# A 7x7 dynamic convolution by frequencies: three image chunks in place of five, four products for 52 frequencies, and the first filter layer applied to the image

## What is computed

```python
key = einsum('bchw,oc->bohw', x, K_w) + K_b              # 49 maps
key = softmax(key.reshape(b, 49, hw).transpose(0, 2, 1), axis=1)   # over pixels
filters = einsum('bcn,bnk->bck', x, key)                  # 128 x 49 for each image
filters = einsum('bck,oc->bok', filters, conv0_w) + conv0_b
filters = (filters - mean) * rsqrt(var + 1e-5) * ln_w + ln_b       # over channels and taps
filters = einsum('bck,oc->bok', relu(filters), conv1_w) + conv1_b
out = depthwise 7x7 convolution of x with filters, padded by 3     # added to the residual
```

## Time and profile before

| | us |
|---|---|
| median of 3 runs | 397.93 |
| lowest and highest | 397.83, 399.51 |
| the profiled execution | 398.06 |
| its span, first to last instruction | 395.9 |
| TensorE, VectorE, ScalarE, GpSimd busy | 378.3, 259.8, 290.4, 154.8 |

### The profile page before, as it was taken

One profiled execution on the slowest core, in us unless ns is written; L12 is line 12 of the kernel. 1 busy time (PEld: TensorE's weight loads), 2 busy tenths in 40 slices (PEclk: granted clock), 3 DMA queues, 4 the chain that ended last, 5 costly groups with the idle time before them and its releaser, 6 DMA issues.

```text
span 395.9 us, 5145 instructions
## 1 busy us (share of the span) xinstructions
PE 378.3 (96%) x1661; PEld 274.1 (69%) x1665; DVE 259.8 (66%) x570; ACT 290.4 (73%) x516; POOL 154.8 (39%) x134
## 2 busy tenths in 40 slices
PE   8999989989999999999999999999999999989895
PEld 2688856444557687877787677877777767656684
DVE  0755556964433865686774995757957497776776
ACT  4552446924204877978979889999899998887883
POOL 5413000910097447121575873121233366332235
PEclk9999999999999999999999999999999999999999
DMA  7960000000000043803110022043030012120232
GB/s 260 447 212 1 2 0 0 2 0 0 2 0 0 3 159 127 352 2 117 35 36 26 2 73 62 28 122 143 5 131 26 29 26 78 58 63 17 81 107 82
DMA packets 11019, 28.90 MB, mean 73 GB/s; under 512 B 1246, under 2 KB 2526, under 8 KB 10736
## 3 DMA queue, kind: packets, MB, share of 16 engines
q1 hardware_dynamic: 10992, 28.58, 21.4%
HBM read 27.95 MB, written 0.62 MB: 72 GB/s over the span
## 4 chain that ended last, share of the span: by engine, by line
PE 67%; ACT 15%; DVE 14%; issue 3%; POOLq 0%; POOL 0%; DVEq 0%
PE ps L435 17%; PE ps L436 16%; PE ps L437 16%; ACT hidh L1076 4%; ACT ps L1077 4%; PE ps L442 3%; PE ps L734 2%; PE ps L447 2%; DVE hidl L1442 2%; PE ps L673 1%; ACT rstd L963 1%; DVE bot L1359 1%; ACT rstd L965 1%; PE ps L458 1%; DVE small L1358 1%
## 5 line engine op out<-in xcount | busy, mean ns | idle before, releaser
L1442 DVE TENSOR_TENSOR hidl<-ps,hidh 128x512 fp32r<-128x512 f32 x160 | 108.4, 687 | 52.9 <-ACT ps L1077 51.5
L406 POOL TENSOR_TENSOR x<-x,parts 128x512 f32<-128x512 f32 x43 | 55.9, 1301 | 147.7 <-DVE parts L1452 96.9
L435 PE MATMUL ps<-xh,wh_all 128*128 128x512 f32 x160 | 74.2, 464 | 2.2 <-DVE hidl L1442 1.7
L1076 ACT ACTIVATE hidh<-ps,par 128x512 fp32r<-128x512 f32 x96 | 68.2, 711 | 8.5 <-PE ps L437 6.8
L435 PE MATMUL ps<-hidh,wh_all 128*128 128x512 f32 (+1 forms) x162 | 64.3, 397 | 4.1 <-DVE hidl L1442 3.8
L1077 ACT ACTIVATE ps<-ps,par 128x512 f32<-128x512 f32 x96 | 65.5, 682 | 0.0
L436 PE MATMUL ps<-xh,wl_all 128*128 128x512 f32 x160 | 63.4, 396 | 0.0
L436 PE MATMUL ps<-hidh,wl_all 128*128 128x512 f32 (+1 forms) x162 | 63.3, 391 | 0.0
L437 PE MATMUL ps<-hidl,wh_all 128*128 128x512 f32 (+1 forms) x162 | 63.1, 390 | 0.0
L437 PE MATMUL ps<-xl,wh_all 128*128 128x512 f32 x160 | 63.0, 394 | 0.0
L396 POOL TENSOR_TENSOR wl_all<-wa,wh_all 128x512 fp32r<-128x512 f32 x40 | 51.3, 1301 | 3.8 <-issue 0.5
(11 more groups left out here) (252 smaller groups left out, 584.2 us busy)
## 6 DMA issues: line engine op xcount, KB each, us to landing
scores_all<-rows_scratch SPq DMA_DIRECT2D x48, 256.0 KB, 3.4
wa<-in_moe SPq DMA_DIRECT2D x2, 4096.0 KB, 15.3
wa<-in_moe SPq DMA_DIRECT2D x1, 2048.0 KB, 9.7
dft_x<-in_dft_x SPq DMA_DIRECT2D x1, 640.0 KB
dft_o<-in_dft_o SPq DMA_DIRECT2D x1, 640.0 KB
w<-in_w_out SPq DMA_DIRECT2D x1, 576.0 KB, 6.8
cst<-in_consts SPq DMA_DIRECT2D x1, 512.5 KB, 5.9
x<-in_x SPq DMA_DIRECT2D x2, 256.0 KB, 2.9
```

Source lines behind the costliest of these rows:

```text
L406: pool.tensor_tensor(half(x, h), half(x, h), parts[:, n % 2, :], ALU.add).then_inc(s["state_added"], 1)
L435: pe.matmul(o, wh, xhi, start=start, stop=False)
L1076: act.activation(hidh[:, n % 2, f, :], sums, func, bias=bias).then_inc(s["hidden_hi_act"], 1)
L1442: dve.tensor_tensor(hidl[:, n % 2, f, :], bank(sums_bank(n, f)), f32(hidh[:, n % 2, f, :]), ALU.subtract).then_inc(s["hidden_lo"], 1)
```

## The change

The spectrum of the image is now kept once, as 128 real parts, 128 imaginary parts, and a third chunk with the other 52 real parts, the constant and the other 52 imaginary parts: three chunks (`XF`), six pieces. For the first 128 frequencies the complex product still takes three real ones; the sum of real and imaginary part that it needs is made by GpSimd from the first two chunks in SBUF, as a fourth chunk of `img_f`. For the other 52 frequencies four real products are taken, in two chunks that both use the third image chunk. So the filters' spectrum, the products and the way back still have five chunks.

The first filter layer is applied to the turned image, since the keys' weighting is linear: `img_w` is `xn` times `conv0_w`, tile by tile, eight matmuls in banks 3 and 6, copied out by ScalarE and VectorE. Line 693 takes `img_w` for `img_t`, and lines 1407 and 698 are gone. The three `keep_clock` matmuls ahead of the first piece are gone too; the zero fill of `filt_two` moves ahead of line 1400.

```diff
-QF = -(-(1 + 3 * FREQ) // C)
+QF = 5
+XF = 3
...
+            pool.wait_ge(s["img_freq_kept"], 2)
+            pool.tensor_tensor(img_f[:, XF, :], img_f[:, 0, :], img_f[:, 1, :], ALU.add).then_inc(s["img_freq_sum"], 1)
             pool.wait_ge(s["filt_act"], 2)
             pool.wait_ge(s["moe1_loaded"], 16)
...
-            keep_clock(3, 3)
-            pe.wait_ge(s["img_ready_act"], 1)
-            pe.wait_ge(s["img_ready_dve"], 1)
-            pe.wait_ge(s["dft_loaded"], 64)
-            img_pieces(0)
-
+            for t in range(TT):
+                if t == 4:
+                    pe.wait_ge(s["img_ready_act"], 1)
+                last = pe.matmul(bank(3 if t < 4 else 6, cols=C, first=t % 4 * C), xn[:, t * C:(t + 1) * C], p("conv0_w"),
+                                 start=True, stop=True)
+                if t % 4 == 3:
+                    last.then_inc(s["first_layer"], 1)
             pe.wait_ge(s["key_diag"], 1)
...
-            img_pieces(1)
+            pe.wait_ge(s["img_ready_dve"], 1)
+            pe.wait_ge(s["dft_loaded"], 64)
+            img_pieces(0)
             pe.wait_ge(s["key_ready"], 1)
+            pe.wait_ge(s["first_kept_act"], 1)
+            pe.wait_ge(s["first_kept_dve"], 1)
             for b in range(B):
                 for j in range(2):
-                    last = pe.matmul(bank(5, cols=KK, first=b * KK), img_t[:, 2 * b + j, :], key_t[:, 2 * b + j, :],
+                    last = pe.matmul(bank(5, cols=KK, first=b * KK), img_w[:, 2 * b + j, :], key_t[:, 2 * b + j, :],
                                      start=(j == 0), stop=(j == 1))
             last.then_inc(s["filt_done"], 1)
-            img_pieces(2)
-            pe.wait_ge(s["filt_in"], 1)
-            pe.matmul(bank(6, cols=B * KK), p("conv0_w"), filt[:, 0].rearrange("p b k -> p (b k)"),
-                      start=True, stop=True).then_inc(s["filt0_done"], 1)
-            for i, numbers in enumerate([(3,), (4, 5)]):
+            for i, numbers in enumerate([(1,), (2,)]):
                 img_pieces(*numbers)
                 pe.wait_ge(s["stat_in"], i + 1)
...
-            img_pieces(6, 7)
+            img_pieces(3, 4)
             pe.wait_ge(s["filt_act"], 2)
...
-            img_pieces(8, 9)
+            img_pieces(5)
...
-            pe.wait_ge(s["img_freq_kept"], QF)
+            pe.wait_ge(s["img_freq_kept"], XF)
...
-            for q in range(QF):
+            act.wait_ge(s["first_layer"], 1)
+            act.activation(img_w[:, 0:4, :].rearrange("p t c -> p (t c)"), bank(3), ACT.Copy).then_inc(s["first_kept_act"], 1)
+            for q in range(XF):
                 act.wait_ge(s["img_freq"], q + 1)
-                act.activation(img_f[:, q, :], bank(q % 4), ACT.Copy).then_inc(s["img_freq_kept"], 1)
-                if q == 2:
+                act.activation(img_f[:, q, :], bank(q), ACT.Copy).then_inc(s["img_freq_kept"], 1)
+                if q == 0:

                     act.wait_ge(s["stat_sum"], 2)
...
+            dve.wait_ge(s["first_layer"], 2)
+            dve.tensor_copy(img_w[:, 4:8, :].rearrange("p t c -> p (t c)"), bank(6)).then_inc(s["first_kept_dve"], 1)
+            step(dve.memset(filt_two[:, :, KK:KEYS - KK], 0.0))
             dve.wait_ge(s["key_turned"], 1)
...
-            dve.tensor_copy(flat(f0), bank(5, cols=B * KK)).then_inc(s["filt_in"], 1)
-            step(dve.memset(filt_two[:, :, KK:KEYS - KK], 0.0))
-            dve.wait_ge(s["filt0_done"], 1)
-            step(dve.tensor_scalar(flat(f1), bank(6, cols=B * KK), p("conv0_b"), None, ALU.add))
+            dve.wait_ge(s["filt_done"], 1)
+            step(dve.tensor_scalar(flat(f1), bank(5, cols=B * KK), p("conv0_b"), None, ALU.add))
...
-            for q in range(QF):
+            dve.wait_ge(s["img_freq_kept"], XF)
+            dve.wait_ge(s["img_freq_sum"], 1)
+            for q, chunk in enumerate((XF, 0, 1, 2, 2)):
                 dve.wait_ge(s["filt_freq"], q + 1)
-                dve.wait_ge(s["img_freq_kept"], q + 1)
-                dve.tensor_tensor(prod_f[:, q, :], bank([5, 6, 7, 4][q % 4]), img_f[:, q, :], ALU.mult).then_inc(s["freq_mult"], 1)
+                dve.tensor_tensor(prod_f[:, q, :], bank([5, 6, 7, 4][q % 4]), img_f[:, chunk, :], ALU.mult).then_inc(s["freq_mult"], 1)
```

More of the change, by code:

```diff
@@ L98 @@
     "picked", "picked_turned", "combined", "combined_turned", "x2_ready",
-    "keys_done", "key_max", "key_exp", "key_diag", "key_turned", "key_ready", "img_turned", "img_ready_act", "img_ready_dve",
-    "filt_done", "filt_in", "filt0_done", "stat_in", "stat_sum", "filt_rstd_ln", "filt_rstd", "filt_act", "filt1_done", "filt1_ready",
+    "keys_done", "key_max", "key_exp", "key_diag", "key_turned", "key_ready", "img_turned", "img_ready_act", "img_ready_dve", "first_layer", "first_kept_act", "first_kept_dve", "img_freq_sum",
+    "filt_done", "stat_in", "stat_sum", "filt_rstd_ln", "filt_rstd", "filt_act", "filt1_done", "filt1_ready",
     "img_freq", "img_freq_kept", "filt_freq", "freq_mult", "img_back", "x3_ready",
@@ L128, in metaformer @@
         wa = sb("wa", [C, E, 1024])
-        dft_x = sb("dft_x", [C, 2, QF * C])
+        dft_x = sb("dft_x", [C, 2, XF * C])
         dft_k = sb("dft_k", [KEYS, QF * C])
@@ L162, in metaformer @@
             filt_t = sb("filt_t", [KEYS, B * C], scope=scope)
-            img_f = sb("img_f", [C, QF, B * C], scope=scope)
+            img_f = sb("img_f", [C, XF + 1, B * C], scope=scope)
+            img_w = sb("img_w", [C, TT, C], scope=scope)
             prod_f = sb("prod_f", [C, QF, B * C], scope=scope)
@@ L670, in img_pieces @@
                     q, j = divmod(n, 2)
-                    if n == 8:
-                        pe.wait_ge(s["img_freq_kept"], 1)
-                    ins = pe.matmul(bank(q % 4), dft_x[:, j, q * C:(q + 1) * C],
+                    ins = pe.matmul(bank(q), dft_x[:, j, q * C:(q + 1) * C],
                                     img_t.rearrange("p (b j) c -> p j b c", j=2)[:, j], start=(j == 0), stop=(j == 1))
@@ L1398, in _ @@
             dve.tensor_tensor(key_d[:], again(ident[0:KK, 0:KK], B), over(krs, KK), ALU.mult).then_inc(s["key_diag"], 1)
+            dve.wait_ge(s["first_layer"], 2)
+            dve.tensor_copy(img_w[:, 4:8, :].rearrange("p t c -> p (t c)"), bank(6)).then_inc(s["first_kept_dve"], 1)
+            step(dve.memset(filt_two[:, :, KK:KEYS - KK], 0.0))
             dve.wait_ge(s["key_turned"], 1)
             dve.tensor_copy(key_t.rearrange("p t k -> p (t k)"), bank(4, cols=TT * KK)).then_inc(s["key_ready"], 1)
-            dve.wait_ge(s["filt_done"], 1)
             f0, f1, f2 = [filt[:, j] for j in range(3)]
@@ L1783, in constants, with chunk, main, rest @@
     ar, ai, br, bi = np.cos(ta), -np.sin(ta), np.cos(tk), np.sin(tk)
[L1784 to L1791, removed]
-    re, im = 2 * ar, 2 * ai
-    back = rows(np.ones((PIX, 1)), re + im, im, -re).T / GRID ** 2
+    re, im = 2 * ar, 2 * ai
+    def chunk(*parts):
+        n = parts[0].shape[0]
+        cols = sum(q.shape[1] for q in parts)
+        return np.concatenate([*parts, np.zeros((n, C - cols))], 1)
+    def main(t):
+        return t[:, :C]
+    def rest(t):
+        return t[:, C:]
+    one = np.ones((PIX, 1))
+    to_x = np.concatenate([main(ar), main(ai), chunk(rest(ar), one, rest(ai))], 1)
+    to_k = np.concatenate([main(br), main(bi - br), main(br + bi), chunk(rest(br), np.ones((KK, 1)), rest(bi)),
+                           chunk(rest(bi), np.zeros((KK, 1)), rest(br))], 1)
+    back = np.concatenate([main(re + im), main(im), main(-re), chunk(rest(re), one, rest(-re)),
+                           chunk(rest(im), 0 * one, rest(im))], 1).T / GRID ** 2
     f32 = np.float32
@@ L1796, in constants @@
         "consts": packed,
-        "dft_x": np.ascontiguousarray(to_x.reshape(2, C, QF * C).transpose(1, 0, 2)).astype(f32),
+        "dft_x": np.ascontiguousarray(to_x.reshape(2, C, XF * C).transpose(1, 0, 2)).astype(f32),
         "dft_k": np.ascontiguousarray(to_k).astype(f32),
```

## The result

| | before | after |
|---|---|---|
| median of 22 runs each, taken beside each other (us) | 398.73 | 396.14 |
| lowest | 397.80 | 394.48 |
| the profiled execution | 398.06 | 396.52 |
| its span | 395.9 | 394.5 |

The ratio is 0.9949, with an interval of 0.9932 to 0.9966: faster by half a per cent. The ratios here leave out the slowest executions (five of before near 404 us, one of after at 400.84), which the medians include; what slows these, and others at a mean granted clock of 0.99 or less by 2 to 6 us, no profile here shows. The medians differ by 2.59 us; the two profiled executions by 1.54.

The account below looks back on a forecast made before the run. It took the chain of waits through the stage (about 94 to 125 us) as the bound, despite TensorE being 96% busy; 1.27 + 0.69 + 0.9 - 0.05 = 2.8 us off 397.93 gave 395.1, range 394.5 to 396.9.

Parts of the forecast that it names:

- case A: Second rectifying instruction gets ahead of GpSimd's sum, so the whole 2.8 us is gained: 395.1 us (394.6 to 395.7), chance 0.50.
- (a): Filter chain: the bias add reads line 693's result directly, without the copy and `conv0_w` matmul between; gain 1.27 us.
- (b): Second statistics matmul and logarithm: one image piece ahead instead of two, no copy pending on ScalarE; gain 0.69 us.
- (c): First filter transform (line 718): one image piece ahead of it instead of two; gain about 0.9 of 0.99 us.
- (d): TensorE: two already met waits before line 693, and line 718's first weight load no longer hidden; cost 0.05 us (0 to 0.1).
- The covers: Added work stays hidden: first layer with 0.1 to 0.3 us spare, last image chunk 0.35, GpSimd's sum 1.9.
- The doubtful place: GpSimd's sum against line 1423's second rectifying instruction on the shared port; the latter ahead by 0.02 to 0.10 us.
- B: GpSimd's sum goes first and blocks rectifying, 1.15 us onto the path, 1.65 gained: 396.3 us (395.8 to 396.8), chance 0.36.
- The prediction's own test: First product, stage end and span must all move 2.8 us; if only the first does, gain is lost behind the stage.
- D: Fewer fillers let TensorE's clock fall to half within the stage, so slower: 398.5 us or more, chance 0.05.
- C: Most gain given back: first layer overruns, last chunk late, or expert stage no earlier; 0.9 us gained, 397.0, chance 0.09.
- signs of being wrong: A key matmul (line 686) later than 96.7 us, or a granted clock under 1.00, would make the prediction wrong.

Follow-up runs that it names:

- The first experiment: Changed kernel with the zero fill of `filt_two` moved between scaling and rectifying, so VectorE asks after GpSimd's sum; stage 28.87 us, 1.30 more than the changed kernel.
- the halves of this change: Kernel before with only the three image chunks (sum late): stage 28.91 us, 1.44 less; with only the first layer on the image: 30.91, 0.56 more.

## Why the prediction was right, and where it was off

It forecast 395.1 with a range of 394.5 to 396.9; it came to 396.14. The traces show case A, and the working of the stage held:

- (a), forecast 1.27. With the two waits of (d) it is 6.13 - 4.79 = 1.34: the release by the filter matmul is 0.04 (101.65 to 101.69) where 0.10 was taken, and the two met waits cost nothing that shows.
- (b), forecast 0.69. From the last squares' sum (104.14) to the logarithm (104.61) it is 0.47, as forecast; the logarithm is 2.02 earlier behind the key matmul (9.73 before, 7.71 after), so (b) is 0.68.
- (c), forecast 0.9 of 0.99. The first filter transform starts 0.06 behind `filt_t` (108.42 to 108.48). The timeline of before has that start at 111.16, where the chain has 111.22, so on equal terms the gap was 0.93 and 0.87 of it was gained.
- (d), forecast 0.05. From `filt_t`'s end to the first product it is 1.32 after and 112.31 - 110.23 = 2.08 before: (c) and (d) together gave 0.76, where 0.85 was forecast. That leaves 0.11 between the transform's start and the product, where the prediction put the unhidden weight load: at its bound of 0.1. No row shows that load's cost by itself. With the 0.03 that (c) lacks it cancels what (a) gave more.
- The sum is 2.77 to the first product and 2.78 to the first expert, for 2.8.
- The covers held, some barely. The first layer ended at 96.63, 0.27 ahead of the key matmul; the last chunk was kept at 109.19 (forecast 109.15); the sum ran from 106.25 to 107.63 (forecast 106.1 and 107.6).
- The doubtful place fell to A: the second rectifying instruction ended at 106.50. Taking 0.17 (0.43 - 0.26) between the two starts, it started at 106.24, 0.01 ahead of GpSimd; 0.02 to 0.10 was forecast, with an error as large. The first experiment shows the price of B, 1.11 for 1.15.

The number alone would have misled, and that the range held is in part luck: 396.14 lies outside A's own range (394.6 to 395.7) and inside B's (395.8 to 396.8), which is what widened the range. Of the miss of 1.0, 0.80 is the starting median: the 397.93 from which the sum started was of 3 runs and low, 398.73 being the median of 22. The other 0.21 is a median gain of 2.59 for 2.8.

What did not hold in the profiled execution is the last step, that the stage's end and the span both come 2.8 earlier: everything behind the stage was taken as moved. The prediction's own test for this, a first product that is 2.8 earlier and a span that is not, came out as a gain given back behind the stage. The prediction had a fall to half clock in D only, in the stage, and a loss behind the stage in C only, by other causes; neither had the place. Two of its signs of being wrong appeared for other reasons: the key matmul came at 96.90, but the normalized input ahead of it was already 0.19 later (line 1236 at 92.01, the old 1230 at 91.82), and the clock under 1.00 lies 225 us behind the stage. The stage kept its clock, and 1.28 us of the profiled execution went to a half clock behind an idle time that the kernel before has too. I had read the page of before, where the clock was at nine tenths or more throughout, as a property of the kernel; it was one of that execution. The runs with fillers show it: with the idle times filled, the kernels differ by 2.73.

The Trainium skill's warning, page "TensorE: Matmul & The Clock Gate", section "Why this matters for your kernels", is of idle gaps between bursts of matmuls. It does not decide this case: its rule does not name a gap like this one, and the clock fell behind it all the same in some executions (0.66 behind an idle time of 1.61 us) and not in others (1.00). Why the clock falls in one execution and not in another is open, and so is whether the change alters how often.

## What to carry to other kernels

Work that runs in a hop of the critical chain has to go before the hop is worth removing: apart, the halves of this change gave 1.44 and -0.56 us, together 2.78. Where two engines want one port, order them by a wait if the later has time to spare; here that costs nothing and takes away a margin of 0.01 us. And a gain that arrives intact at the end of its stage is still in front of every idle gap behind it: look for the longest, and for what makes it, since one profiled execution can pass it at full clock and the next not.

## What was not expected of the hardware

A margin of 0.01 us, worked out as above, repeats. In three executions GpSimd's sum started 0.18 us behind the first rectifying instruction (106.07 and 106.25, 106.34 and 106.52, and 105.73 and 105.91 with the fillers), and VectorE won each time; both sides hang on the second statistics matmul. The clock does not repeat: behind the same idle time of 1.60 to 1.61 us the granted clock at 350 to 355 us was 0.66 in both profiles of the changed kernel, 0.84 and 0.72 in those of the first layer alone and of the three chunks with the early sum, and 1.00 in the one with the sum last, in the one with the zero fill moved, in the three chunks with the late sum and in the kernel before.
